# Near keys of linear attention: high and low scores in one matmul of 512 columns, and a sum of two bank halves over 256 columns

## The chip, the core and the metric

The kernel runs on one NeuronCore of one Trainium2 chip. The metric is the device time of one execution in microseconds (us). Each time below is that of one program launch; the profile is one more execution, taken by the hardware profiler.

## What is computed

The input has 4 sequences of 256 tokens with 512 features. A linear attention with 32 heads of 128 features follows, then a sigmoid gate with RMS norm, an output projection, a layer norm, a small mixture of low-rank experts beside a dense layer, and a second layer norm. The part that matters here, per head and batch:

```python
qkv = silu(hidden @ qkv_w.T)                       # q, k, v of each head, 128 features
scores = einsum('bhnd,bhmd->bhnm', cq, ck) * diag_decay   # in blocks of 32 tokens
intra  = einsum('bhnm,bhmd->bhnd', scores, cv)
inter  = einsum('bhnd,bhde->bhne', cq * q_decay, kv)      # kv: the running state
attn   = intra + inter
xf = attn * rsqrt(mean(attn * attn) + EPS)         # over all heads of a token
out = sigmoid(hidden @ gate_w.T) * norm_w * xf @ out_w.T
```

The kernel doesn't keep the running state. A batch has 256 tokens, so it makes the whole decayed score matrix of a head: 128 near keys against 256 queries and 128 far keys against the last 128 queries.

## The kernel before

**Precision.** Every fp32 product is made from two parts of each operand, a rounded high part and the rest as low part, with three matmuls: high by high, high by low, low by high. ScalarE makes the high parts (helper `copy`, L471, or `silu`, L517), VectorE the low ones (helper `minus`, L1179). So each engine has a piece of work for each operand, and TensorE waits for the low part.

**Blocks.** The 32 heads are worked in 8 groups of 4. A group has blocks named QK0, V0, V1, G01, QK1, G23, QK2, QK3 (query and key projection of one head, values of four, gates of two) and, after V1, the output projection of the group before. Each block is a Strassen-like product of seven terms, `p1` to `p7`, made by `mm3_onto` (L2013 to L2015). Its results go to banks 0 to 3 of PSUM. The attention of a head is woven between the products of the next blocks, in banks 4 to 7, one bank for a batch. It is done in two halves, `e` = 0 and 1, of two batches each.

**The path of a head's half.** `scores(h, e)` on TensorE (L2104 to L2110), decay mask on VectorE (L1251, L1253, L1259), high part on ScalarE and low part on VectorE (both 128x768), then `attention(h, e)` on TensorE: five matmuls a batch. The first three (`mm3`, L2007 to L2009) multiply the near keys' values by the scores of all 256 queries and write columns 0 to 255 of the bank. The fourth (L2124) multiplies the far keys' high values by high and low scores side by side and writes columns 128 to 383: the low part lands in 256 to 383, beside the result. The fifth (L2126) adds the low values. Then a chain of four steps brings the result together:

- ScalarE, `part(h, e)`: copies columns 256 to 383 of both banks into the buffer `sq` (in the profile L471, `sq<-ps 128x256`). It waits for `att_done` of TensorE and for `sq_added` of GpSimd, because `sq` is still being read by the half before.
- VectorE, `add_part(h, e)` (L1268): adds `sq` to columns 128 to 255 of both banks.
- ScalarE, `square(h, e)` (L629): squares the 512 results into the same `sq`. GpSimd adds them to `sqacc` (L1927, `add_squares`), which frees `sq`.
- VectorE, `gated(h, e)` (L1280; L1532 in the last group): multiplies by the gate into `y`, which raises `y_done`. `scores` of the next head into these banks wait for it.

**Queues.** The order on each engine is written out by hand, block by block (functions `qk0`, `v0`, `v1`, `qk1`, ... for each engine), and each engine works its list strictly in order. In `qk1` and `qk2` ScalarE has after `part(h, 1)` the copy of the next head's values (`values_hi`, L471, `vh<-v`), the silus of the next head's q and k, and `square(h, 1)`. VectorE has `add_part(h, 1)`, the low values (`values_lo`, `vl<-v,vh`), the sums `c22_add` and `c12_add` (L1209, L1218), `gated(h, 1)` and the low parts of k (`k1_low`, `k0_low`), for which the next `scores(h + 1, 0)` wait. GpSimd makes the sums of weight blocks for the Strassen terms (L1884, L1887, L1891) from what DMA brings, and `add_squares` in between. `v0` and `v1` have `add_part` of the group's last head ahead of `sums_lo(g, "oa", "A")`, and a little later `sums_lo(g, "ob", "A")`, for which the output projection waits.

Of the kernel before, what the change touches and what calls it, by code (L numbers as in the profile page):

```python
# [14 lines left out]
P = 128  # L15
BATCH, SEQ, HID = 4, 256, 512
# [6 lines left out]
W = 512  # L23
U = 256
SC = SEQ + P
# [96 lines left out]
def added_no(g, name, j):  # L122

    return len(OUT_ADDS) * (g - 1) + OUT_ADDS.index((name, j)) + 1
# [26 lines left out]
def build(nc, stream, xt, x, decay, norm_w, base_b, lora_router, router_b, expert_map, ident_in, ones_in, fresh_in, out):  # L151
    ctx = ExitStack()
    with ctx:
        def sb(name, shape, dt=FP32):
            return ctx.enter_context(nc.sbuf_tensor(name, shape, dt))

        def sem(name):
            return ctx.enter_context(nc.semaphore(name))
# [11 lines left out]
        vh = sb("vh", [P, TT, P], FP32R)  # L170
        vl = sb("vl", [P, TT, P], FP32R)
        s2 = sb("s2", [P, 2, BATCH, SC], FP32R)
        sh, sl = s2[:, 0, :, :], s2[:, 1, :, :]
# [8 lines left out]
        sq = sb("sq", [P, W])  # L182
# [90 lines left out]
        att_part, att_full = sem("att_part"), sem("att_full")  # L273
# [28 lines left out]
        def att_banks(e, c0, c1):  # L302

            return ps[:, S_B + 2 * e:S_B + 2 * e + 2, c0:c1]

        def by_batch(ap):
            return ap.rearrange("p (b n) -> p b n", b=2)
# [161 lines left out]
        def _(act):  # L469
            def copy(dst, src, **kw):  # L470
                return nc.scalar.activation(dst, src, ACT.Copy, **kw)  # L471

            def sums_hi(g, name, part):

                m = load_no(g, name)
                act.wait_ge(t_sum, load_no(g, name) - 2)
                wait_free(act, g, name, part)
                u0, u1 = (0, 3) if part == "A" else (3, 7)
                runs = pieces(g, name, u0, u1)
                for i, (slot, before, n) in enumerate(runs):  # L480
                    ins = copy(wh[:, slot:slot + n, :], stage[:, m % 2, u0 + before:u0 + before + n, :])
                    if i == len(runs) - 1:
                        ins.then_inc(t_hi, 1)
# [138 lines left out]
            def part(h, e):  # L622
                act.wait_ge(att_done, 2 * h + e + 1)
                act.wait_ge(sq_added, 2 * h + e)
                copy(by_batch(sq[:, 0:SEQ]), att_banks(e, SEQ, SC)).then_inc(att_part, 1)

            def square(h, e):
                act.wait_ge(att_full, 2 * h + e + 1)
# [158 lines left out]
            def qk0(g):  # L787
                n, h = block_no(g, QK0), HG * g
                k0_full(n - 1, h - 1)
                u2_copy(n)  # L790
                q1_out(n - 1, h - 1)
                k1_full(n - 1, h - 1)
                part(h - 2, 0)
                p5_copy(n)
                square(h - 2, 0)
                u3_copy(n)
                sums_hi(g, "vb", "A")
                part(h - 2, 1)
                values_hi(h - 1)
                square(h - 2, 1)  # L800
                sums_hi(g, "va", "B")
                q0_out(n, h)
                sums_hi(g, "vb", "B")
                scores_hi(h - 1, 0)
                k1_out(n, h)
# [370 lines left out]
        def _(dve):  # L1176
# [88 lines left out]

            def add_part(h, e):
                dve.wait_ge(att_part, 2 * h + e + 1)
                nc.vector.tensor_tensor(att_banks(e, P, SEQ), att_banks(e, P, SEQ), by_batch(sq[:, 0:SEQ]), ALU.add)\  # L1268
                    .then_inc(att_full, 1)

            def gated(h, e):
# [117 lines left out]
            def qk0(g):  # L1389
                n, h = block_no(g, QK0), HG * g  # L1390
                k0_low(n - 1, h - 1)
                add_part(h - 2, 0)
                q1_low(n - 1, h - 1)
                gated(h - 2, 0)
                k1_low(n - 1, h - 1)
                sums_lo(g, "vb", "A")
                add_part(h - 2, 1)
                gated(h - 2, 1)
                mask(h - 1, 0)
                c22_add(n)  # L1400
                mask_sum(h - 1, 0)
                sums_lo(g, "va", "B")
                c12_add(n)
                values_lo(h - 1)
                scores_lo(h - 1, 0)
                sums_lo(g, "vb", "B")

            def v0(g):
                n, h = block_no(g, V0), HG * g
                q0_low(n - 1, h)  # L1410
                mask(h - 1, 1)
                k1_low(n - 1, h)
                mask_sum(h - 1, 1)
                k0_low(n - 1, h)
                q1_low(n - 1, h)
                scores_lo(h - 1, 1)
                add_part(h - 1, 0)
                c22_add(n)
                gated(h - 1, 0)
                c12_add(n)  # L1420
# [583 lines left out]
        def _(pe):  # L2004
            def mm3(dst, wt, mv_, start, stop):

                nc.tensor.matmul(dst, wt[0], mv_[0], start=start, stop=False)  # L2007
                nc.tensor.matmul(dst, wt[0], mv_[1], start=False, stop=False)  # L2008
                return nc.tensor.matmul(dst, wt[1], mv_[0], start=False, stop=stop)  # L2009
# [103 lines left out]
            def attention(h, e):  # L2113
                pe.wait_ge(v_lo, h + 1)
                pe.wait_ge(s_lo, 2 * h + e + 1)
                if h > 0 and h % HG == 0:
                    pe.wait_ge(o_added, added_no(h // HG, "c21" if e else "c12", 1))
                for b in (2 * e, 2 * e + 1):
                    bank = ps[:, S_B + b, :]
                    mm3(bank[:, 0:SEQ], (vh[:, 2 * b, :], vl[:, 2 * b, :]),  # L2120
                        (sh[:, b, 0:SEQ], sl[:, b, 0:SEQ]), True, False)


                    nc.tensor.matmul(bank[:, P:SC], vh[:, 2 * b + 1, :], s2[:, :, b, SEQ:SC],  # L2124
                                     start=False, stop=False, skip_group_check=True)
                    last = nc.tensor.matmul(bank[:, P:SEQ], vl[:, 2 * b + 1, :], sh[:, b, SEQ:SC],  # L2126
                                            start=False, stop=True)
                last.then_inc(att_done, 1)

            def out_product(g, i, j, bank, start, stop):  # L2130
# [102 lines left out]
            def qk0(g):  # L2233
                n, h = block_no(g, QK0), HG * g
                p1(n)
                p4(n - 1)
                attention(h - 2, 0)
                p5(n)
                p6(n)
                attention(h - 2, 1)  # L2240
                p2(n)
                scores(h - 1, 0)
                p7(n)
                p3(n)
                scores(h - 1, 1)

            def v0(g):
                n, h = block_no(g, V0), HG * g
                p1(n)
                p4(n - 1)  # L2250
                p5(n)
                p6(n)
                if g > 0:
                    attention(h - 1, 0)
                p2(n)
                p7(n)
                p3(n)
# [374 lines left out]
```

## Time and profile before

| | us |
|---|---|
| median of 3 runs | 996.95 |
| lowest and highest | 996.23, 997.51 |
| the profiled execution | 996.55 |
| its span | 994.8 |

| engine | busy, us | share | instructions |
|---|---|---|---|
| TensorE, matmuls (PE) | 982.2 | 99% | 5569 |
| TensorE, weight loads (PEld) | 860.6 | 87% | 5569 |
| VectorE (DVE) | 815.9 | 82% | 1122 |
| ScalarE (ACT) | 710.0 | 71% | 1197 |
| GpSimd (POOL) | 456.0 | 46% | 426 |

The granted clock of TensorE was 0.998 of full speed over the span. In the rows, a matmul's duration runs from its issue to its modelled end, so matmuls that follow each other overlap: what one costs in a full queue is the distance from its start to the start of the next. A row's name is output <- inputs, a form is output size <- input size; the line of a copy is that of its helper (L471 for all plain ScalarE copies). 1.6 to 1.8 us of an execution lie outside the span.

### The profile page before, as it was taken

Reading aid. Unit: us, or ns where it says so; the run is one execution under the profiler, and the core shown is the slowest. Engines: PE = TensorE matmul, PEld = TensorE weight load, DVE = VectorE, ACT = ScalarE, POOL = GpSimd, SP = SyncE. Lnnn points to the kernel's source line nnn. Section 1 sums busy time; section 2 is a strip of 40 time slices with the busy share of each in tenths; the row PEclk is TensorE's granted clock in tenths of the full one; section 3 lists DMA queues with packets and bytes.
Section 4 is the critical chain, followed back from the end, with each engine's and each line's share of the span. In section 5 each row is a group of like instructions: output and inputs, shape, how many; then the busy total and the mean of one; then the engine's idle time right before and its main releaser. Section 6 shows DMA issues by size and latency. Waiting matters only on the chain.

```text
span 994.8 us, 15911 instructions
## 1 busy us (share of the span) xinstructions
PE 982.2 (99%) x5569; PEld 860.6 (87%) x5569; DVE 815.9 (82%) x1122; ACT 710.0 (71%) x1197; POOL 456.0 (46%) x426
## 2 busy tenths in 40 slices
PE   8999999999999999999999999999999999999997
PEld 7878998889888898889988898888988899888896
DVE  6767887888967988779877889778887788899876
ACT  6677885788767785778857887677857788587653
POOL 1352564446453463534644464544635345531423
PEclk9999999999999999999999999999999999999999
DMA  6121111201121112212112111110122121110402
GB/s 211 30 64 46 64 48 48 71 30 52 51 65 51 35 47 72 63 44 66 45 55 66 30 52 51 64 51 30 51 72 64 38 73 38 56 52 22 159 12 85
DMA packets 52799, 57.78 MB, mean 58 GB/s; under 512 B 4336, under 2 KB 47728, under 8 KB 52720
## 3 DMA queue, kind: packets, MB, share of 16 engines
q1 hardware_dynamic: 52720, 56.77, 18.3%
q8 instruction: 45, 0.74, 0.3%
q14 instruction: 34, 0.28, 0.1%
HBM read 54.65 MB, written 2.10 MB: 57 GB/s over the span
## 4 chain that ended last, share of the span: by engine, by line
PE 93%; DMA 1%; ACT 1%; DVE 1%; issue 1%; POOL 1%; SPq 0%; POOLq 0%; ACTq 0%; DVEq 0%
PE ps L2013 25%; PE ps L2014 24%; PE ps L2015 24%; PE ps L2007 3%; PE ps L2009 3%; PE ps L2008 3%; PE ps L2110 2%; PE ps L2104 2%; PE ps L2106 2%; PE ps L2105 1%; PE ps L2124 1%; DMA stage<-stream 1%; PE ps L2108 1%; PE ps L2126 1%; DVE wl L1179 1%
## 5 line engine op out<-in xcount | busy, mean ns | idle before, releaser
L1884 POOL TENSOR_TENSOR stage<-stage 128x512 f32<-128x512 f32 x75 | 106.6, 1421 | 354.6 <-DMA stage<-stream 290.8
L2013 PE MATMUL ps<-xh,wh 128*128 128x512 f32 x658 | 260.0, 395 | 1.4 <-ACT stg L517 1.0
L2014 PE MATMUL ps<-xl,wh 128*128 128x512 f32 x658 | 257.0, 391 | 0.0
L2015 PE MATMUL ps<-xh,wl 128*128 128x512 f32 x658 | 256.2, 389 | 0.0
L1179 DVE TENSOR_TENSOR wl<-stage,wh 128x768 fp32r<-128x768 f32 (+3 forms) x183 | 201.3, 1117 | 28.4 <-ACT wh L471 27.7
L471 ACT ACTIVATE wh<-stage 128x768 fp32r<-128x768 f32 (+3 forms) x183 | 147.4, 833 | 17.8 <-POOL stage L1891 8.1
L2015 PEld LDWEIGHTS ps<-xh,wl 128*128 128x128 f32 x658 | 123.6, 188 | 26.8
L2013 PEld LDWEIGHTS ps<-xh,wh 128*128 128x128 f32 x658 | 123.7, 188 | 25.4 <-issue 1.8
L1927 POOL TENSOR_TENSOR sqacc<-sqacc,sq 128x512 f32<-128x512 f32 x64 | 92.8, 1451 | 110.9 <-ACT sq L629 110.9
L2014 PEld LDWEIGHTS ps<-xl,wh 128*128 128x128 f32 x658 | 123.7, 188 | 21.9
L471 ACT ACTIVATE ps<-ps 128x512 f32<-128x512 f32 x150 | 87.0, 584 | 65.0 <-PE ps L2015 65.0
L2013 PE MATMUL ps<-wh,xh 128*128 128x256 f32 (+1 forms) x423 | 122.8, 290 | 0.0
L2015 PE MATMUL ps<-wh,xl 128*128 128x256 f32 (+1 forms) x423 | 121.7, 288 | 0.0
L2014 PE MATMUL ps<-wl,xh 128*128 128x256 f32 (+1 forms) x423 | 121.5, 287 | 0.0
L1891 POOL TENSOR_TENSOR stage<-stage 128x256 f32<-128x256 f32 x75 | 81.0, 1080 | 5.9
L2013 PEld LDWEIGHTS ps<-wh,xh 128*128 128x128 f32 x423 | 80.8, 191 | 0.4
L2014 PEld LDWEIGHTS ps<-wl,xh 128*128 128x128 f32 x423 | 80.9, 191 | 0.3
L2015 PEld LDWEIGHTS ps<-wh,xl 128*128 128x128 f32 x423 | 80.8, 191 | 0.0
L1887 POOL TENSOR_TENSOR stage<-stage 128x256 f32<-128x256 f32 x75 | 68.4, 912 | 5.9
L1179 DVE TENSOR_TENSOR s<-ps,s 128x768 fp32r<-128x768 f32 x64 | 61.0, 953 | 10.1 <-ACT s L471 9.9
L471 ACT ACTIVATE s<-ps 128x768 fp32r<-128x768 f32 x64 | 51.7, 808 | 22.3 <-DVE ps L1259 22.2
L1253 DVE TENSOR_TENSOR ps<-ps,dec 128x768 f32<-128x768 f32 x64 | 61.1, 955 | 0.0
(224 smaller groups left out, 2320.9 us busy)
## 6 DMA issues: line engine op xcount, KB each, us to landing
stage<-stream SPq DMA_DIRECT2D x75, 384.0 KB, 3.4
stage<-stream SPq DMA_DIRECT2D x79, 128.0 KB, 2.1
dec<-decay SPq DMA_DIRECT2D x32, 192.0 KB, 2.4
stage<-stream SPq DMA_DIRECT2D x13, 256.0 KB, 3.1
acc<-xt SPq DMA_DIRECT2D x8, 256.0 KB, 6.0
v<-x SPq DMA_DIRECT2D x8, 256.0 KB, 5.8
out<-v SPq DMA_DIRECT2D x8, 256.0 KB, 2.0
y_home<-lora_router SPq DMA_DIRECT2D x1, 512.0 KB, 5.1
```

The lines of the kernel that those rows point to most:

```text
L471: return nc.scalar.activation(dst, src, ACT.Copy, **kw)
L1179: return nc.vector.tensor_tensor(dst, full, f32(hi), ALU.subtract)
L1253: nc.vector.tensor_tensor(att_banks(e, 0, SC), att_banks(e, 0, SC), dec[:, h % 2, :].unsqueeze(1).broadcast_to([P, 2, SC]), ALU.mult)\
L1884: nc.gpsimd.tensor_tensor(stage[:, s, 1:5:3, :], stage[:, s, 0:6:5, :], stage[:, s, 7:8, :].broadcast_to([P, 2, U]), ALU.add).then_inc(t_p ...
L1887: nc.gpsimd.tensor_tensor(stage[:, s, 2, :], stage[:, s, 1, :], stage[:, s, 5, :], ALU.add)\
L1891: nc.gpsimd.tensor_tensor(stage[:, s, 6, :], stage[:, s, 2, :], stage[:, s, 3, :], ALU.add)\
L1927: nc.gpsimd.tensor_tensor(sqacc[:, e, :], sqacc[:, e, :], sq[:, :], ALU.add).then_inc(sq_added, 1)
L2007: nc.tensor.matmul(dst, wt[0], mv_[0], start=start, stop=False)
L2008: nc.tensor.matmul(dst, wt[0], mv_[1], start=False, stop=False)
L2013: nc.tensor.matmul(dst, wt[0], mv_[0], start=start, stop=False, skip_group_check=True)
L2014: nc.tensor.matmul(dst, wt[0], mv_[1], start=False, stop=False, skip_group_check=True)
L2015: return nc.tensor.matmul(dst, wt[1], mv_[0], start=False, stop=stop, skip_group_check=True)
```

## The change

It touches the attention's matmuls, the copy `part` and the sum `add_part`.

- TensorE: the three matmuls on near keys become two. The first has 512 columns: the high values by high and low scores side by side, into the whole bank, high into 0 to 255 and low into 256 to 511. The second adds the low values by the high scores into 0 to 255. The far keys' matmul of 256 columns now writes two pieces of 128 columns, 128 to 255 and 384 to 511. The last is as before. In all four matmuls a batch instead of five, with the same 1152 columns.
- ScalarE: `part` copies 256 columns of each of two banks, 512 in all, instead of 256 in all.
- VectorE: `add_part` adds 512 columns instead of 256.

```diff
@@ ScalarE
             def part(h, e):
                 act.wait_ge(att_done, 2 * h + e + 1)
                 act.wait_ge(sq_added, 2 * h + e)
-                copy(by_batch(sq[:, 0:SEQ]), att_banks(e, SEQ, SC)).then_inc(att_part, 1)
+                copy(by_batch(sq[:, :]), att_banks(e, SEQ, W)).then_inc(att_part, 1)
@@ VectorE
             def add_part(h, e):
                 dve.wait_ge(att_part, 2 * h + e + 1)
-                nc.vector.tensor_tensor(att_banks(e, P, SEQ), att_banks(e, P, SEQ), by_batch(sq[:, 0:SEQ]), ALU.add)\
+                nc.vector.tensor_tensor(att_banks(e, 0, SEQ), att_banks(e, 0, SEQ), by_batch(sq[:, :]), ALU.add)\
                     .then_inc(att_full, 1)
@@ TensorE, attention(h, e)
                 for b in (2 * e, 2 * e + 1):
                     bank = ps[:, S_B + b, :]
-                    mm3(bank[:, 0:SEQ], (vh[:, 2 * b, :], vl[:, 2 * b, :]),
-                        (sh[:, b, 0:SEQ], sl[:, b, 0:SEQ]), True, False)
-
-
-                    nc.tensor.matmul(bank[:, P:SC], vh[:, 2 * b + 1, :], s2[:, :, b, SEQ:SC],
+                    parts = bank.rearrange("p (a n) -> p a n", a=2)
+                    nc.tensor.matmul(parts, vh[:, 2 * b, :], s2[:, :, b, 0:SEQ], start=True, stop=True)
+                    nc.tensor.matmul(bank[:, 0:SEQ], vl[:, 2 * b, :], sh[:, b, 0:SEQ], start=False, stop=False,
+                                     skip_group_check=True)
+                    nc.tensor.matmul(parts[:, :, P:SEQ], vh[:, 2 * b + 1, :], s2[:, :, b, SEQ:SC],
                                      start=False, stop=False, skip_group_check=True)
                     last = nc.tensor.matmul(bank[:, P:SEQ], vl[:, 2 * b + 1, :], sh[:, b, SEQ:SC],
-                                            start=False, stop=True)
+                                            start=False, stop=True, skip_group_check=True)
```

TensorE's list before, around an attention half in a V0 block; the second batch begins in the last row.

```order
L2015 MATMUL ps<-wh,xl 128x256
L2007 MATMUL ps<-s,vh 128x256 [waits s_lo,v_lo]
L2008 MATMUL ps<-s,vh 128x256
L2009 MATMUL ps<-s,vl 128x256
L2124 MATMUL ps<-s,vh 128x256
L2126 MATMUL ps<-s,vl 128x128
L2007 MATMUL ps<-s,vh 128x256
```

The same place now.

```order
L2015 MATMUL ps<-wh,xl 128x256
L2121 MATMUL ps<-s,vh 128x512 [waits s_lo,v_lo]
L2122 MATMUL ps<-s,vl 128x256
L2124 MATMUL ps<-s,vh 128x2x128
L2126 MATMUL ps<-s,vl 128x128
L2121 MATMUL ps<-s,vh 128x512
```

Nothing else moved on TensorE; each attention half is two instructions shorter. On ScalarE and VectorE the lists stand as before, and only the size in the rows of `part` (`sq<-ps`, now 128x512) and of `add_part` (L1268, now 128x2x256) differs.

## Rows read from the trace of the kernel before

**Rows 1.** The page, part 1: busy time, share of the span, instructions.
```profile
PE 982.2 (99%) x5569; PEld 860.6 (87%) x5569; DVE 815.9 (82%) x1122; ACT 710.0 (71%) x1197; POOL 456.0 (46%) x426
```

**Rows 2.** Timeline of PE: start, duration (us), engine, line, operation, names, form.
```profile
53.04 0.39 PE L2013 MATMUL ps<-xh,wh 128*128 128x512 f32 x1
...
53.72 0.28 PE L2007 MATMUL ps<-s,vh 128*128 128x256 f32 x1
...
54.20 0.22 PE L2126 MATMUL ps<-s,vl 128*128 128x128 f32 x1
54.26 0.34 PE L2007 MATMUL ps<-s,vh 128*128 128x256 f32 x1
54.43 0.28 PE L2008 MATMUL ps<-s,vh 128*128 128x256 f32 x1
...
54.85 0.45 PE L2013 MATMUL ps<-xh,wh 128*128 128x512 f32 x1
55.13 0.40 PE L2014 MATMUL ps<-xl,wh 128*128 128x512 f32 x1
```

**Rows 3.** Groups by line and form, whole span: count | busy us, mean ns.
```profile
L629 ACT ACTIVATE sq<-ps 128x512 f32<-128x512 f32 x64 | 38.3, 599 | 21.3 <-DVE ps L1268 21.2
L1209 DVE TENSOR_TENSOR stg<-ps,stg 128x512 f32<-128x512 f32 x61 | 41.7, 684 | 14.7 <-PE ps L2015 14.7
L1268 DVE TENSOR_TENSOR ps<-ps,sq 128x256 f32<-128x256 f32 x64 | 27.5, 430 | 39.9 <-ACT sq L471 39.6
L471 ACT ACTIVATE sq<-ps 128x256 f32<-128x256 f32 x64 | 24.4, 382 | 25.8 <-POOL sqacc L1927 18.4 <-PE ps L2126 7.4
```

**Rows 4.** Timelines of ACT, POOL, DVE and PE, block QK1 of group 2.
```profile
291.88 0.39 ACT L471 ACTIVATE sq<-ps 128x256 f32<-128x256 f32 x1 [1.26 <-POOL sqacc L1927]
...
292.65 1.30 POOL L1884 TENSOR_TENSOR stage<-stage 128x512 f32<-128x512 f32 x1 [0.86 <-DMA stage<-stream]
...
293.25 1.78 DVE L1179 TENSOR_TENSOR vl<-v,vh 128x1024 fp32r<-128x1024 f32 x1 [0.52 <-ACT vh L471]
...
297.35 1.89 DVE L1179 TENSOR_TENSOR k<-stg,k 128x512 fp32r<-128x512 f32 x2
...
297.53 0.63 ACT L517 ACTIVATE stg<-stg 128x512 f32<-128x512 f32 x1
...
299.34 0.35 PE L2104 MATMUL ps<-q,k 128*128 128x256 f32 x1
```

**Rows 5.** Timelines of POOL, DVE and PE, block QK1 of group 4.
```profile
525.78 1.23 DVE L1179 TENSOR_TENSOR vl<-v,vh 128x1024 fp32r<-128x1024 f32 x1 [0.52 <-ACT vh L471]
...
525.83 1.78 POOL L1887 TENSOR_TENSOR stage<-stage 128x256 f32<-128x256 f32 x1
...
529.45 1.88 DVE L1179 TENSOR_TENSOR k<-stg,k 128x512 fp32r<-128x512 f32 x2
...
531.66 0.28 PE L2104 MATMUL ps<-q,k 128*128 128x256 f32 x1
```

**Rows 6.** Timelines of POOL and DVE, block V1 of group 3.
```profile
359.74 0.43 DVE L1268 TENSOR_TENSOR ps<-ps,sq 128x256 f32<-128x256 f32 x1 [1.61 <-ACT sq L471]
...
361.06 1.29 POOL L1906 TENSOR_TENSOR y<-y,y_home 128x512 f32<-128x512 f32 x1
...
361.57 1.60 DVE L1179 TENSOR_TENSOR wl<-stage,wh 128x768 fp32r<-128x768 f32 x1
```

**Rows 7.** Timelines of DVE and PE, block QK0 of group 6.
```profile
692.50 0.69 DVE L1280 SCALAR_TENSOR_TENSOR y<-y,ps 128x512 f32<-128x512 f32 x1 [0.67 <-ACT sq L629]
...
693.34 0.36 PE L2104 MATMUL ps<-q,k 128*128 128x256 f32 x1 [0.18 <-DVE y L1280]
```

**Rows 8.** Timelines of DVE and PE, the last block of the last group.
```profile
919.46 0.43 DVE L1268 TENSOR_TENSOR ps<-ps,sq 128x256 f32<-128x256 f32 x1
...
919.80 0.68 DVE L1209 TENSOR_TENSOR stg<-ps,stg 128x512 f32<-128x512 f32 x1
...
920.86 0.39 PE L2013 MATMUL ps<-xh,wh 128*128 128x512 f32 x1
```

## The prediction

> **What bounds the kernel now.** I read the page's busy times first, then TensorE's timeline in steady stretches for what a matmul costs in a full queue, then the groups by line and form for the two instructions that grow, and last, for each wait of TensorE, the timelines of the engines that it waits for. TensorE is busy for 982.2 of 994.8 us, VectorE for 815.9, ScalarE for 710.0 [rows 1]. So TensorE's list is the time: a matmul less is a gain at once, and work added to another engine costs only where TensorE already waits for it, or comes within a few tenths of a microsecond of doing so. The reader should see two things in the rows: the pace of TensorE, and how little room there is at a handful of places.
>
> **The gain: one matmul fewer a batch.** Start to start, three matmuls of 512 columns take 53.72 - 53.04 = 0.68 us, 0.227 each. The four of 256 columns from 53.72 to 54.20 take 0.12 each, the one of 128 takes 0.06 [rows 2]. So 512 columns in one piece cost 0.227, in two pieces 0.24: the merge gives 0.013 us. A head has four batches: 32 x 4 = 128 merges, 1.7 us. The first matmul after the one of 128 columns costs 0.05 more (54.26 to 54.43, 0.17 instead of 0.12); one of 512 columns in that place also costs 0.05 more (54.85 to 55.13, 0.28 instead of 0.227) [rows 2]. That cancels. The far keys' matmul has the same 256 columns, but writes two pieces with a gap between. No row of TensorE shows such an output. Its bounds are nothing, as for a contiguous one of 256, and the 0.05 us of the nearest irregularity, which would be 128 x 0.05 = 6.4 us. A gain is excluded, since the columns are the same. I take nothing, because the input side of this same matmul already comes in two pieces and keeps the pace of 0.12.
>
> The Trainium skill says in "TensorE: Matmul & The Clock Gate", section "Back-to-back issue gap", that an isolated warm matmul takes N / 2.4 + 2.5 ns. By that a merge saves 2.5 ns, 0.3 us in all, and the forecast would come out 1.4 us higher. The row shows 13 ns, and I go by the row.
>
> **The cost: two longer steps in each half.** There are 64 halves. ScalarE's `part` takes 0.382 us for 256 columns; its square of 512 columns from PSUM into the same buffer takes 0.599 [rows 3]. I take 0.58 to 0.60: +0.20 us, 13 us of ScalarE over the kernel. VectorE's `add_part` takes 0.430; a sum of 512 columns with one input in PSUM takes 0.684 [rows 3]: +0.25 us, 16 us of VectorE. The link from `att_done` to the squares grows by 0.45 us. And since `part` of half 1 waits until GpSimd has added the squares of half 0, a delay of half 0 is handed on to half 1 through GpSimd: there it can reach 0.45 + 0.20 = 0.65 before `add_part`. If all of it came through at the places below, it would cost about 8 us; all of it hidden, nothing. What decides is what else the delayed instructions are waiting for.
>
> **Block QK1, where scores wait for the low part of k.** `part(h, 1)` starts at 291.88, released by GpSimd's squares; the copy of the values follows it, and VectorE's `values_lo` starts at 293.25, released by that copy [rows 4]. From there VectorE is busy without a gap up to `k0_low`, the second of the two at 297.35, which ends at 299.24; the scores start at 299.34 [rows 4]. So TensorE waits for this chain, and `values_lo` would start some 0.5 us later (0.3 handed on through the squares, 0.2 from the copy). But `values_lo` takes 1.78 us here and 1.23 in group 4 [rows 4, 5]. GpSimd's L1884 runs from 292.65 to 293.95, released by a DMA, and VectorE's instruction stands still behind it. A start at 293.75 instead of 293.25 then ends at the same time. What is left is ScalarE: its last silu of k ends at 298.16 [rows 4], 0.4 us before `k0_low` starts (299.24 - 0.68 = 298.56); 0.5 later makes 0.1 us. So I take 0.1 in group 2 and nothing in group 1, which looks alike with a little more room.
>
> In groups 0, 3 and 6 `sums_hi` is late for another reason (its sums come late from GpSimd), so nothing is handed on and only the longer copy, 0.2 us, reaches `k0_low`, through ScalarE: 0.2 each. Group 4 goes the other way. `values_lo` starts at 525.78, 0.05 ahead of GpSimd's L1887 at 525.83, and makes that wait: 1.78 us [rows 5]. Half a microsecond later GpSimd is first, and VectorE waits for it: about 0.9 us, of which the following blocks of GpSimd give some back. I take 0.6; `k0_low` ends at 531.33 and the scores start at 531.66, so 0.25 us is room [rows 5]. That leaves 0.3. Group 5 has `values_lo` just ahead of GpSimd too, but its `k0_low` is itself held up by GpSimd later, which takes the delay up: nothing. The last group has this block in another order, 0.2. Sum: 0.1 + 3 x 0.2 + 0.3 + 0.2 = 1.2 us. Block QK2 has the same chain with 0.5 us of room: 0.2 us for all groups.
>
> The Trainium skill says in "SBUF — State Buffer", section "Who interferes with whom", that VectorE and GpSimd share an exclusive pair of ports and that the one which issues second stands fully still. By that rule the trace agrees: 1.78 us against 1.23 for the same instruction.
>
> **Start of the output projection.** It waits for `sums_lo(g, "ob", "A")` on VectorE, some 10 us after `add_part` of the group's last half (359.74), with hardly a gap between [rows 6]. By then the delays of both halves have added up to some 0.9 us. `sums_lo(g, "oa", "A")` at 361.57 takes 1.60 us because GpSimd's L1906 runs until 362.35 [rows 6]; started at 362.5, it loses only about 0.25, and the few idle tenths before the next steps take that up. I take 0.1 us for each of six groups. In group 7 the two engines meet the other way around, and I take 0.85, the full delay. Sum 1.45 us.
>
> **Single places.** In group 6 the scores of block QK0 wait for `gated`, which ends at 693.19 and releases TensorE at 693.34; ahead of it stand `add_part` and the square [rows 7]. The +0.25 of `add_part` passes whole: 0.26. In the last block `c22_add` stands behind `add_part` of the last half: it starts at 919.80 and ends at 920.48, and TensorE needs it at 920.86 [rows 8]. The delay there is the handed-on 0.45, plus 0.20, plus 0.25: 0.9 us, less 0.34 of room: 0.56. Two halves earlier another 0.16. Sum 1.0 us.
>
> **The sum.** -1.7 + 1.2 + 0.2 + 1.45 + 1.0 = +2.1 us. On the profiled execution's 996.55 that is 998.7; the median of the runs is 0.4 higher, so I forecast **999.1 us**, 0.2% above.
>
> **The rivals.**
> *All hidden.* Between the attention and the next wait stand GpSimd locks and DMA waits that set the end of VectorE's work anyway. For it: groups 1 and 5 and the start of the output projection in most groups. Against it: rows 7 and 8, where no such lock stands. With the last block's costs alone it is 996.95 - 1.7 + 1.0 = 996.3; without these 995.3.
> *Not swallowed (slower).* The delays of 0.45 to 0.65 pass whole, because VectorE comes behind GpSimd instead of ahead of it as in group 4. The place is `values_lo` in QK1 and `sums_lo(g, "oa", "A")` in V1. Price: 0.5 x 8 in QK1, 0.35 x 7 at the projection, single places 1.5: 8 - 1.7 = +6.3, 1003.2 us. It decides from the point where `values_lo` starts after GpSimd's next step has begun: rows 4 have 0.7 us of that step left, rows 5 none.
> *The scattered output costs.* At 0.05 us a matmul the gain of 1.7 becomes a loss of 4.7: 1005.5. Nothing in the trace speaks for it.
> *Not what it says.* That TensorE keeps five matmuls is excluded by the order of instructions.
>
> **Chances.** Forecast with its own range 997.5 to 1001: 0.45. All hidden, 995.2 to 997.5: 0.28. Not swallowed, 1001 to 1006: 0.22. Scattered output or something else: 0.05. A measurement of this kernel can tell about 0.2% from no change, 2.0 us: below 994.9 is faster, above 998.9 slower. Faster would need more than the whole 1.7 us: 0.06. Slower: a little over half of the forecast's case, all of the third, most of the last: 0.50. The same: 0.44. For 8 in 10 the range takes in most of the second and third cases: 995.6 to 1003.5.
>
> **What would show it.** In the changed profile: TensorE's matmuls 128 fewer; L2121 at 0.22 to 0.28 start to start and the scattered L2124 at 0.12; `part` at 0.58 to 0.60 and `add_part` at 0.68 us. `values_lo` in QK1 of group 2 should end when it does now, relative to the attention before it, and be shorter by its later start; in group 4 it should be longer, about 1.7. The waits of the scores L2104 should grow by 1 to 2 us in all, and the last block's L2013 should start 0.5 us late after its predecessor. I am wrong if L2124 shows 0.17, if `add_part` stays well below 0.6, or if waits of TensorE grow by more than 5 us or shrink.

## The result, and the profile after

| | before | after |
|---|---|---|
| median, us | 996.96 (4 runs) | 1005.92 (4 runs) |
| lowest and highest | 996.23, 997.51 | 1005.38, 1006.95 |
| span of the profiled execution | 994.8 | 1004.7 |

The ratio is 1.0094 (95% interval 1.0082 to 1.0107): 0.9% slower, 9.0 us. The forecast was 999.1 with a range up to 1003.5.

The page of the changed kernel, busy times, and from its groups by line and form the two longer steps (third and fourth row), their two neighbours, and the group of TensorE's matmuls that begin a product of 256 columns:

```profile
PE 988.3 (98%) x5441; PEld 855.6 (85%) x5441; DVE 828.9 (83%) x1122; ACT 723.1 (72%) x1197; POOL 450.5 (45%) x426
```

```profile
L629 ACT ACTIVATE sq<-ps 128x512 f32<-128x512 f32 x64 | 38.4, 601 | 28.9 <-DVE ps L1268 28.8
...
L1209 DVE TENSOR_TENSOR stg<-ps,stg 128x512 f32<-128x512 f32 x61 | 41.7, 683 | 13.9 <-PE ps L2015 13.9
...
L1268 DVE TENSOR_TENSOR ps<-ps,sq 128x512 f32<-128x512 f32 x64 | 44.6, 696 | 49.8 <-ACT sq L471 49.8
...
L471 ACT ACTIVATE sq<-ps 128x512 f32<-128x512 f32 x64 | 38.2, 596 | 26.4 <-POOL sqacc L1927 19.0 <-PE ps L2126 7.1
...
L2013 PE MATMUL ps<-wh,xh 128*128 128x256 f32 x392 | 112.8, 288 | 4.6 <-ACT ps L471 4.6
```

TensorE has 128 matmuls fewer. `part` takes 0.596 us instead of 0.382, `add_part` 0.696 instead of 0.430 [rows 3]: both as forecast. The last row is the news: TensorE now stands 4.6 us for a ScalarE copy at the begin of a product in the value blocks. No row of that kind and size stood in the profile before.

TensorE's timeline of an attention half in a full queue, with what begins behind it:

```profile
290.20 0.39 PE L2121 MATMUL ps<-s,vh 128*128 128x512 f32 x1
290.43 0.28 PE L2122 MATMUL ps<-s,vl 128*128 128x256 f32 x1
290.54 0.28 PE L2124 MATMUL ps<-s,vh 128*128 128x256 f32 x1
290.66 0.22 PE L2126 MATMUL ps<-s,vl 128*128 128x128 f32 x1
290.72 0.46 PE L2121 MATMUL ps<-s,vh 128*128 128x512 f32 x1
291.01 0.28 PE L2122 MATMUL ps<-s,vl 128*128 128x256 f32 x1
...
291.31 0.45 PE L2013 MATMUL ps<-xh,wh 128*128 128x512 f32 x1
```

The scattered L2124 costs 0.12 start to start, like a contiguous one. But the half takes 291.31 - 290.20 = 1.11 us, against 54.85 - 53.72 = 1.13 before [rows 2]; over all halves the medians are 1.113 and 1.123. The merged matmul costs 0.23 behind one of 512 columns and 0.29 behind the one of 128, where the two of 256 before cost 0.17 + 0.12 = 0.29 too. So the merges give 0.01 a half, 0.6 to 0.8 us in all, not 1.7.

Where the time went is read by how much later TensorE comes by in the changed kernel. It jumps in one block above all. Block V1 of group 3, timelines of GpSimd, VectorE, ScalarE and TensorE (compare [rows 6]):

```profile
364.89 1.29 POOL L1906 TENSOR_TENSOR y<-y,y_home 128x512 f32<-128x512 f32 x1
366.14 1.30 POOL L1884 TENSOR_TENSOR stage<-stage 128x512 f32<-128x512 f32 x1
```

```profile
364.05 0.70 DVE L1268 TENSOR_TENSOR ps<-ps,sq 128x512 f32<-128x512 f32 x1 [1.83 <-ACT sq L471]
...
366.15 2.11 DVE L1179 TENSOR_TENSOR wl<-stage,wh 128x768 fp32r<-128x768 f32 x1
368.18 0.41 DVE L1251 TENSOR_TENSOR ssum<-ps,dec 128x256 f32<-128x256 f32 x1
...
374.10 1.75 DVE L1179 TENSOR_TENSOR wl<-stage,wh 128x768 fp32r<-128x768 f32 x1
```

```profile
369.97 0.81 ACT L471 ACTIVATE s<-ps 128x768 fp32r<-128x768 f32 x1 [1.69 <-DVE ps L1259]
370.67 0.59 ACT L471 ACTIVATE ps<-ps 128x512 f32<-128x512 f32 x1
```

```profile
370.47 0.28 PE L2015 MATMUL ps<-wh,xl 128*128 128x256 f32 x1
371.32 0.39 PE L2013 MATMUL ps<-wh,xh 128*128 128x256 f32 x1 [0.57 <-ACT ps L471]
...
375.91 0.50 PE L2013 MATMUL ps<-yh,wh 128*128 128x512 f32 x1
```

GpSimd in the kernel before, behind the L1906 of [rows 6]:

```profile
362.31 2.01 POOL L1884 TENSOR_TENSOR stage<-stage 128x512 f32<-128x512 f32 x1
```

Before, `sums_lo(g, "oa", "A")` came to VectorE at 361.57, while GpSimd's L1906 ran until 362.35, and took 1.60 us [rows 6]. It was ahead of L1884, and L1884 took 2.01 instead of 1.30. Now it comes at 366.15, 0.01 us after GpSimd has begun its next instruction, L1884, and takes 2.11. Decay mask, ScalarE's `scores_hi` (idle for 1.69 until then) and, behind that on ScalarE, the copy `u3_copy` follow; TensorE's `p7` waits for it: it starts at 371.32, where a full queue would start it 0.12 behind the matmul at 370.47, at 370.59. Then the output projection starts at 375.91, released by the low sums of ob that end at 375.85. Counted in TensorE's progress, `p7` costs 0.82 us in each of six groups and 1.3 in the last one, the projection's start 0.24 in six: 6 x 0.82 + 1.3 + 6 x 0.24 = 7.7 us. The prediction had 1.45 there. In the last group the two engines meet otherwise, and the full delay passes.

The single places, timelines of VectorE and TensorE: block QK0 of group 6, then the last block [rows 7, 8].

```profile
699.32 0.69 DVE L1280 SCALAR_TENSOR_TENSOR y<-y,ps 128x512 f32<-128x512 f32 x1 [0.66 <-ACT sq L629]
...
700.15 0.35 PE L2104 MATMUL ps<-q,k 128*128 128x256 f32 x1 [0.96 <-DVE y L1280]
```

```profile
929.87 0.68 DVE L1209 TENSOR_TENSOR stg<-ps,stg 128x512 f32<-128x512 f32 x1
...
930.61 0.50 PE L2013 MATMUL ps<-xh,wh 128*128 128x512 f32 x1 [0.49 <-DVE stg L1209]
```

TensorE's wait in group 6 is 0.96 instead of 0.18: 0.78 more. The last block costs 0.78, and the scores two halves earlier 0.70.

### The profile page after: what moved, and what is told of

Read it like the earlier page. It is cut to its first block and busy times, and to the rows that moved or that the text cites. A ratio compares the mean times of both kernels' runs of the same rounds, so it can differ in the third digit from the quotient of the medians.

```text
span 1004.7 us, 15655 instructions
## 1 busy us (share of the span) xinstructions
PE 988.3 (98%) x5441; PEld 855.6 (85%) x5441; DVE 828.9 (83%) x1122; ACT 723.1 (72%) x1197; POOL 450.5 (45%) x426
## 5 line engine op out<-in xcount | busy, mean ns | idle before, releaser
L1884 POOL TENSOR_TENSOR stage<-stage 128x512 f32<-128x512 f32 x75 | 99.9, 1332 | 358.6 <-DMA stage<-stream 293.2
L1179 DVE TENSOR_TENSOR wl<-stage,wh 128x768 fp32r<-128x768 f32 (+3 forms) x183 | 204.3, 1134 | 24.2 <-ACT wh L471 23.4
L1268 DVE TENSOR_TENSOR ps<-ps,sq 128x512 f32<-128x512 f32 x64 | 44.6, 696 | 49.8 <-ACT sq L471 49.8
L1891 POOL TENSOR_TENSOR stage<-stage 128x256 f32<-128x256 f32 x75 | 80.7, 1076 | 5.9
L1887 POOL TENSOR_TENSOR stage<-stage 128x256 f32<-128x256 f32 x75 | 71.5, 954 | 5.9
```

What stands on the lines that cost most here:

```text
L1179: return nc.vector.tensor_tensor(dst, full, f32(hi), ALU.subtract)
L1268: nc.vector.tensor_tensor(att_banks(e, 0, SEQ), att_banks(e, 0, SEQ), by_batch(sq[:, :]), ALU.add)\
L1884: nc.gpsimd.tensor_tensor(stage[:, s, 1:5:3, :], stage[:, s, 0:6:5, :], stage[:, s, 7:8, :].broadcast_to([P, 2, U]), ALU.add).then_inc(t_p ...
L1887: nc.gpsimd.tensor_tensor(stage[:, s, 2, :], stage[:, s, 1, :], stage[:, s, 5, :], ALU.add)\
L1891: nc.gpsimd.tensor_tensor(stage[:, s, 6, :], stage[:, s, 2, :], stage[:, s, 3, :], ALU.add)\
```

## The experiments

All ratios are to the kernel before on the same chip, with 95% intervals; its medians there were 996.1 to 996.5. The expectations set theory S against others. S (string and threshold) says that delays add up along the lists of ScalarE and VectorE, and that the price jumps where VectorE comes behind GpSimd's next step in V1. Theory A (additive) says that each longer step has a price of its own.

The profiled executions differ by up to 2 us before the first block begins: TensorE's first block matmul starts at 41.41 us in the changed kernel, 41.48 in the kernel before, 42.66 in e7 and 43.09 in e2. Where a cause is in question, the text below therefore goes by TensorE's lag over a stretch of one execution (how much later it comes by at its end than at its begin, against the kernel before), and not by the whole time. From just ahead of `p7` in V1 to the first matmul of the projection the changed kernel loses 1.0 us in each of groups 1 to 6.

| kernel | median, us | ratio |
|---|---|---|
| e1 matmuls alone | 992.62 | 0.9960 (0.9949 to 0.9972) |
| e2 copy alone | 998.55 | 1.0022 (1.0011 to 1.0032) |
| e3 sum alone | 997.61 | 1.0011 (0.9998 to 1.0024) |
| e4 `u3_copy` first | 1005.95 | 1.0097 (1.0078 to 1.0117) |
| e5 mask first | 1004.63 | 1.0076 (1.0061 to 1.0091) |
| e6 mask first, in before | 997.38 | 1.0008 (0.9997 to 1.0019) |
| e7 copy and sum, old matmuls | 1010.31 | 1.0131 (1.0111 to 1.0151) |
| e8 one half of eight short | 999.87 | 1.0037 (1.0023 to 1.0050) |
| e9 only its copy short | 1000.00 | 1.0042 (1.0027 to 1.0057) |
| e10 new in heads 0, 1 | 996.91 | 1.0011 (1.0002 to 1.0020) |
| e11 new in heads 2, 3 | 999.14 | 1.0040 (1.0027 to 1.0054) |
| e12 sums early | 1000.50 | 1.0045 (1.0030 to 1.0060) |
| e13 sums early, keys first | 1005.72 | 1.0102 (1.0085 to 1.0119) |
| e14 both moves, in before | 996.86 | 1.0006 (0.9997 to 1.0015) |

### Which part costs: e1, e2, e3, e7

e1, the changed kernel with short steps:

```diff
-copy(by_batch(sq[:, :]), att_banks(e, SEQ, W)).then_inc(att_part, 1)
+copy(by_batch(sq[:, 0:SEQ]), att_banks(e, SEQ + P, W)).then_inc(att_part, 1)
-tensor_tensor(att_banks(e, 0, SEQ), att_banks(e, 0, SEQ), by_batch(sq[:, :]), ALU.add)
+tensor_tensor(att_banks(e, P, SEQ), att_banks(e, P, SEQ), by_batch(sq[:, 0:SEQ]), ALU.add)
```

> The four new matmuls, with copy and sum as short as before (256 columns: the copy takes columns 384 to 511, the sum adds them to 128 to 255). Left out: the product of high values and low scores of the first 128 queries, which lands in columns 256 to 383 and is added to nothing. If TensorE's part is what the prediction took it for (128 x 0.013 us gained, the scattered output free), the time is 996.95 - 1.7 = 995.3 us (994.5 to 996). If the new matmuls themselves cost something that the pitches don't show, it is above 997. The loss of about 9 us must then come from the two longer steps, or not.

e2 and e3, the kernel before with one step longer each (e2's sum, not shown, reads the same 256 columns as before out of the wider copy):

```diff
@@ e2
-copy(by_batch(sq[:, 0:SEQ]), att_banks(e, SEQ, SC)).then_inc(att_part, 1)
+copy(by_batch(sq[:, :]), att_banks(e, SEQ, W)).then_inc(att_part, 1)
@@ e3
-tensor_tensor(att_banks(e, P, SEQ), att_banks(e, P, SEQ), by_batch(sq[:, 0:SEQ]), ALU.add)
+both = att_banks(e, 0, SEQ).rearrange("p b (a n) -> p b a n", a=2)
+low = by_batch(sq[:, 0:SEQ]).unsqueeze(2).broadcast_to([P, 2, 2, P])
+tensor_tensor(both, both, low, ALU.add)
```

> The kernel before, with only ScalarE's copy lengthened to 512 columns (the sum still uses 256 of them). Theory S (string and threshold): from block QK2 to the start of the projection ScalarE and VectorE hand work to each other with hardly a gap, delays add up, and the low sums of oa in V1 come only 0.2 us later against GpSimd; VectorE is then still first in line when GpSimd's L1906 ends, so no port swap: 998 us (997 to 999.5). Theory A (additive: each of the two longer steps has its own price in proportion to its length): the 10.7 us between 995.3 and 1005.9 split as 0.21 to 0.27, so +4.7: 1001.6 us.

> The kernel before, with only VectorE's sum lengthened to 512 columns; it adds the low part to columns 0 to 127 too, where it does not belong. Theory S: three longer sums lie on the string, so at V1 VectorE is 0.5 us later against GpSimd, less than the 0.75 of the changed kernel and less than the 0.8 that L1906 has left, so VectorE stays first and the 0.5 us of port swap is not paid: about 0.4 a group and 0.6 in the singles, 1000.5 us (999 to 1002). Theory A: +6.0: 1003 us. Under S the effects of copy and sum add up to about 5, well under the 10.7 that both have together; under A they add up to 10.7.

e7 has both longer steps together, with the five old matmuls.

> The kernel before with its five matmuls, and copy and sum both of 512 columns (the sum adds the low part to columns 0 to 127 too, where it does not belong). Alone the copy cost 2.1 us and the sum 1.1, and the matmuls alone gained 3.9, together -0.7; the changed kernel loses 9.4. Theory S: it is the two longer steps together that bring VectorE 0.75 us later against GpSimd in V1, behind the begin of L1884, so that it stands for 1.2 us instead of going first; the five old matmuls don't matter for that: 1006 us (1003 to 1008). Rival M: the interaction is with the new matmuls (TensorE 0.2 us a group earlier uses up the last room), and here the two costs only add up: 999.7 us.

Measured against before: matmuls -3.9 us, copy +2.1, sum +1.1 (its interval reaches from nothing to 2.4); both steps together +14.2, the whole change +9.0. The steps cost far more together than apart: theory A, a price for each, falls, and so does rival M, since e7 has the old matmuls. S had the pattern, but only e2 lies in its range: e1 and e3 came out 2.7 and 2.9 us below the expected time, e7 4.3 above it. e7 shows the stall of V1 to the hundredth. GpSimd, VectorE and TensorE in e7, group 3:

```profile
366.53 1.30 POOL L1908 TENSOR_TENSOR y<-y,y_home 128x512 f32<-128x512 f32 x1
367.79 1.30 POOL L1886 TENSOR_TENSOR stage<-stage 128x512 f32<-128x512 f32 x1
```

```profile
367.80 2.10 DVE L1179 TENSOR_TENSOR wl<-stage,wh 128x768 fp32r<-128x768 f32 x1
```

```profile
372.96 0.38 PE L2015 MATMUL ps<-wh,xh 128*128 128x256 f32 x1 [0.55 <-ACT ps L471]
```

In e3 the same sums arrive before the meeting point, and they take less time than before:

```profile
361.12 1.30 POOL L1908 TENSOR_TENSOR y<-y,y_home 128x512 f32<-128x512 f32 x1
362.36 2.03 POOL L1886 TENSOR_TENSOR stage<-stage 128x512 f32<-128x512 f32 x1
```

```profile
362.17 1.06 DVE L1179 TENSOR_TENSOR wl<-stage,wh 128x768 fp32r<-128x768 f32 x1
```

They arrive 0.60 us later than before by the clock and end at the same time: 362.17 + 1.06 = 363.23, before 361.57 + 1.60 = 363.17. The delay is swallowed, and it is GpSimd's L1886 that waits (2.03 instead of 1.30).

The same place gives the reason for the jump. What counts is how far the sums come ahead of GpSimd's next step: 362.31 - 361.57 = 0.74 us in the kernel before, 0.54 in e2, 0.19 in e3, and nothing in e7 (367.80 against 367.79). The copy takes 0.20 of this room and the sum 0.55, and together they use it up. From `p7` to the start of the projection TensorE loses 0.00 in e2 and e3 in groups 2 to 6, and 1.0 in e7 in each of them. With the last group that is 7.3 of the 14.3 us by which e7's profile is longer; 1.2 stand before the first block, and the rest is spread over QK1, QK2 and the single places.

### Which wait: e4, e5, e6

e4 takes the last link away: ScalarE's copy goes first.

```diff
-scores_hi(h, 0)
 u3_copy(n)
+scores_hi(h, 0)
 sums_hi(g, "ob", "A")
```

> The changed kernel, with ScalarE's u3_copy in V1 ahead of scores_hi(h, 0) instead of behind it; in the profile its input is there 2.5 us before it starts, and TensorE's p7 waits 0.72 us for it. Theory O (order): what costs is that u3_copy stands behind scores_hi, so p7 starts 0.7 us earlier and the kernel gets back 6 x 0.7 + 1.3 = 5.6 us: 1000.3 us. Theory S: p7 starts earlier, but VectorE's list up to the low sums of ob is without a gap from add_part on and ends when it did, so the same wait comes up again at p4 (c22_added) and at the projection's start (t_lo): 1005.5 us (1004.5 to 1006).

1005.95: the time is that of the changed kernel. TensorE's `p7` no longer waits, but two products later it does; TensorE and VectorE in e4, group 3:

```profile
374.31 0.39 PE L2013 MATMUL ps<-wh,xh 128*128 128x256 f32 x1 [0.60 <-DVE stg L1209]
```

```profile
373.58 0.68 DVE L1209 TENSOR_TENSOR stg<-ps,stg 128x512 f32<-128x512 f32 x1
```

VectorE has no gap from 366.24 to 376.79 there. It is its list that is late, and the copy was only where the delay came out first. So the theory "order" (O) falls.

The same execution holds the clearest test of the meeting. In groups 2 and 4 the sums come 0.02 to 0.03 us ahead of GpSimd's step instead of behind it; VectorE and GpSimd in e4, group 2:

```profile
250.02 0.96 DVE L1179 TENSOR_TENSOR wl<-stage,wh 128x768 fp32r<-128x768 f32 x1
```

```profile
250.04 2.10 POOL L1884 TENSOR_TENSOR stage<-stage 128x512 f32<-128x512 f32 x1
```

From `p7` to the start of the projection TensorE loses 0.00 us in these two groups, and 1.0 in each of groups 1, 3, 5 and 6, where the sums take 2.09 to 2.10. The lists are the same in all these groups; what differs is who comes first. The whole time doesn't show the two spared groups: this execution's first block begins 1.1 us later than in the changed kernel's profile, and the output block behind group 4 loses another 0.3.

e5 moves the low sums behind the mask, e6 does so in the kernel before.

```diff
 gated(h - 1, 1)
-sums_lo(g, "oa", "A")
 mask(h, 0)
 mask_sum(h, 0)
+sums_lo(g, "oa", "A")
 operand_lo(g, 5)
```

> The changed kernel, with VectorE's low sums of oa in V1 behind the mask of the next head instead of ahead of it. In the changed kernel these sums arrive at 366.15, just after GpSimd's L1884 has begun at 366.14, and take 2.11 us; mask, scores_hi, u3_copy and TensorE's p7 stand behind them. Theory S (string and threshold): mask starts 2 us earlier, p7 no longer waits (0.72 us in six groups, 1.3 in the last), and the sums themselves meet GpSimd for less time, so that the low sums of ob come 0.5 to 0.9 us earlier: of the 1.08 us a group 0.5 to 1.0 comes back, 1000 us (998.5 to 1002.5). Theory W (the wait only moves, as when u3_copy went first): the low sums of ob end when they did, 1005.5 us.

> The same move in the kernel before, as a control. There p7 has 1.1 us of room and the projection's start 0.16, and VectorE goes first after L1906. Theory S: nothing to gain at p7; the projection's start moves by what the changed meeting with GpSimd gives or takes: 996.5 us (995.5 to 998). If the move were simply better everywhere, it would gain here as much as in the changed kernel: 991 us.

e5 got 1.3 us back of the 6 expected: a miss. The meeting moved on with the sums; VectorE in e5:

```profile
367.12 1.42 DVE L1179 TENSOR_TENSOR wl<-stage,wh 128x768 fp32r<-128x768 f32 x1
368.46 1.75 DVE L1179 TENSOR_TENSOR vl<-y_home,vh 128x1024 fp32r<-128x1024 f32 x1
```

1.42 + 1.75 us for the two instructions that took 2.11 + 1.22 in the changed kernel: 0.16 less. `p7` was free, but `p4` and the projection waited: TensorE lost 0.7 in each group from `p7` to the projection's start, instead of 1.0. e6 was level, as expected.

### Length or meeting point: e8, e9, e12

e8 shortens copy and sum in one half of eight; e9 only the copy there. The edit (shown for the copy) takes eight halves of 64: seven stand right ahead of the meeting in V1, the eighth stands in the last block, where there is no such meeting. The expectations count seven.

```diff
+if h % HG == 3 and e == 1:
+    copy(by_batch(sq[:, 0:SEQ]), att_banks(e, SEQ + P, W)).then_inc(att_part, 1)
+else:
     copy(by_batch(sq[:, :]), att_banks(e, SEQ, W)).then_inc(att_part, 1)
```

> The changed kernel, but in one half of eight (the second of each group's last head, in block V1) copy and sum are as short as before; left out there: the product of high values and low scores of the first 128 queries. 0.48 us less on the string just ahead of the low sums of oa. Theory S: these arrive 0.3 us after GpSimd's L1906 instead of 0.75, are first in line for L1884, and both the 0.5 us of stall and the 0.48 us are gone: 7 x 0.9 = 6 us come back, 1000 us (998.5 to 1001.5). Theory A (each half costs its share of the 9 to 13 us): 7 of 64 halves, 1.0 to 1.5 us back: 1004.7 us.

> The changed kernel; in one half of eight (the second of each group's last head, block V1) ScalarE's copy alone is as short as before, VectorE's sum keeps its 512 columns (in these halves it adds the low part of queries 128 to 255 to columns 0 to 127 too, where it does not belong). This takes the two effects of the last run apart, length and port. Theory S: the low sums of oa arrive 0.54 us late against GpSimd instead of 0.75, before L1906 ends, so they are first in line again and stall no longer than in the kernel before: 0.21 + 0.5 us of 7 groups come back, 1001 us (999.5 to 1002.5). Theory L (length only, no threshold): 7 x 0.21 = 1.5 us back, 1004.5 us.

Both give 6 us back; e9 does so with eight copies 0.23 us shorter (0.37 instead of 0.60), 1.8 us of work. Group 3 of e9, GpSimd and VectorE:

```profile
362.78 1.30 POOL L1913 TENSOR_TENSOR y<-y,y_home 128x512 f32<-128x512 f32 x1
364.04 2.02 POOL L1891 TENSOR_TENSOR stage<-stage 128x512 f32<-128x512 f32 x1
```

```profile
363.82 1.07 DVE L1182 TENSOR_TENSOR wl<-stage,wh 128x768 fp32r<-128x768 f32 x1
```

The sums arrive 0.22 us ahead of GpSimd's next step instead of 0.01 behind it, and take 1.07 instead of 2.11. TensorE loses 0.00 us there in groups 2 to 6 in both, instead of 1.0. That the sum's extra 0.27 makes no difference between e8 and e9 is the swallowing again. (e8's profiled execution, 1002.26, was the longest of its seven.)

e12 shortens nothing. It moves the sums ahead of a GpSimd instruction:

```diff
@@ ScalarE, v1
 part(h - 1, 1)
+sums_hi(g, "oa", "A")
 u2_copy(n)
 square(h - 1, 1)
-sums_hi(g, "oa", "A")
@@ VectorE, v1
-gated(h - 1, 1)
 sums_lo(g, "oa", "A")
+gated(h - 1, 1)
 mask(h, 0)
```

> The changed kernel; in V1 ScalarE makes the high sums of oa right behind the copy, ahead of u2_copy and square, and VectorE the low sums ahead of the gate. Nothing is left out. The low sums then arrive at about 364.75 by the trace of the changed kernel, 0.07 us before GpSimd's L1902 ends and 0.14 before its L1906 would begin, so that VectorE goes first and L1906 and L1884 shift behind it. Theory S (it is the meeting with GpSimd): mask starts 1.5 to 1.8 us earlier, all waits of V1 and at the projection's start go: 7 x 1.08 = 7.5 us back, 998.4 us (997 to 1000.5). Theory W (string length alone sets it, as when the mask went first): 0.3 us a group, 1004 us.

1000.5, 5.4 us back of the 9.0. Group 3, VectorE and GpSimd:

```profile
363.73 0.96 DVE L1179 TENSOR_TENSOR wl<-stage,wh 128x768 fp32r<-128x768 f32 x1
```

```profile
363.84 2.00 POOL L1906 TENSOR_TENSOR y<-y,y_home 128x512 f32<-128x512 f32 x1
```

Undisturbed, the sums take 0.96 us, and TensorE loses 0.00 us at this place in groups 2 to 6. With e4, e9 and e12 the meeting point is shown: in e12 the same work, with only the order of arrival changed, is worth 5.4 us. In the last group e12 still waited at `p4` and the projection. No run has the move of V1 alone in the kernel before; e14 below has it together with another and is level.

### Where the delay comes from: e10, e11

Each has the changed kernel's matmuls, copy and sum in two of a group's four heads and the old ones in the others (`h % HG < 2` in e10, `h % HG > 1` in e11).

> Matmuls, copy and sum of the changed kernel in heads 0 and 1 of each group (blocks QK1 and QK2), those of the kernel before in heads 2 and 3 (QK0, V0, V1). Nothing is left out. Theory S: the loss of V1 needs the longer steps of heads 2 and 3; here only what QK1 and QK2 cost is left, 1.4 us by the prediction, against half of the matmuls' gain, 0.85: 997.5 us (996 to 999). Theory A (each half its share): half of the loss, 1001 us.

> The complement: the changed kernel's steps in heads 2 and 3 (QK0, V0, V1), those of before in heads 0 and 1. Nothing is left out. Theory S: the 0.75 us against GpSimd arise in V0 and V1 alone, so the port swap and most of the string are there: 0.8 to 1.0 us a group in V1, the single places of groups 6 and 7: 1003.5 us (1002 to 1005.5). Theory A: 1001 us. If the delay carried over from QK2 were needed for it, this and the run before would both stay below 999.

e10 is 0.6 us slower than before, as S had it. e11 came to 999.1, not 1003.5: a miss. Its executions spread from 997.2 to 1002.8, and its profile says why. Groups 4 and 5 of the same execution, VectorE and GpSimd each:

```profile
478.32 0.96 DVE L1182 TENSOR_TENSOR wl<-stage,wh 128x768 fp32r<-128x768 f32 x1
```

```profile
478.33 2.11 POOL L1891 TENSOR_TENSOR stage<-stage 128x512 f32<-128x512 f32 x1
```

```profile
595.02 2.12 DVE L1182 TENSOR_TENSOR wl<-stage,wh 128x768 fp32r<-128x768 f32 x1
```

```profile
595.02 1.30 POOL L1891 TENSOR_TENSOR stage<-stage 128x512 f32<-128x512 f32 x1
```

At 0.01 us ahead VectorE takes 0.96 and GpSimd 2.11; at a tie VectorE takes 2.12 and GpSimd 1.30. In all six groups of e11 the two starts lie within 0.01 us of each other. VectorE is first in groups 2, 3 and 4, and TensorE loses 0.00 us there; it is second in groups 1, 5 and 6, and TensorE loses 0.8 to 1.0 (in the seventh group the engines meet otherwise). The starts in the trace don't say who wins so near the edge: group 3 is a tie too, and VectorE takes 0.96. e10 still has 0.72 us of the 0.74 of room. So the steps of heads 2 and 3 use the room up alone, to the very edge, where S had expected them to go past it. In the changed kernel's profile all six groups are past it, by 0.01 to 0.03 us. Heads 0 and 1 matter for that: e11's ten executions lie at 997.2 to 1002.8, the changed kernel's four at 1005.4 to 1007.0. How their steps supply these hundredths no run shows.

### The key blocks: e13, e14

e13 is e12 with the low parts of k ahead of `gated` on VectorE, and ScalarE's high parts of k ahead of the next high sums; e14 has both moves in the kernel before.

```diff
@@ VectorE, qk1 and qk2
 c12_add(n)
-gated(h, 1)
 k1_low(n, h + 1)
 k0_low(n, h + 1)
+gated(h, 1)
@@ ScalarE, qk1 (qk2 alike)
-sums_hi(g, "qk2", "B")
 k1_out(n, h + 1)
 k0_out(n, h + 1)
+sums_hi(g, "qk2", "B")
```

> The kernel of the run before, and in QK1 and QK2 the low parts of k ahead of the gate on VectorE, and the high parts of k ahead of the next high sums on ScalarE. Nothing is left out. If QK1 and QK2 cost what the prediction took for them, 1.4 us, and the kernel before itself waits there in some groups (0.1 to 0.8 us each), this gains 2 to 3 us more: 996 us (994.5 to 998), about the kernel before or a little under. If these waits only move on to V1, it gains nothing: 998.4 us.

> Both moves in the kernel before, as a control. In V1 there is nothing to gain (0.16 us and more of room), in QK1 and QK2 what TensorE waits there: 1 to 2 us: 995 us (993.5 to 997). The difference to the run above then says what the change is worth where its longer steps are covered: between the -1.7 us that the prediction took for the matmuls and the -3.9 us of the matmuls alone, plus the single places of groups 6 and 7.

e13 lost 5.2 us to e12: a miss. TensorE's waits at `k0_lo` shrank by up to 0.2 us each, and one in QK0 grew by 0.8 in nearly every group; TensorE in e13, group 3:

```profile
348.14 0.36 PE L2104 MATMUL ps<-q,k 128*128 128x256 f32 x1 [0.64 <-DVE y L1280]
```

By the rows, ScalarE's sums (1.05 us in QK2) now stand right ahead of `u2_copy` and `q1_out`, and that delay seems to run on through QK3 to `gated` in QK0; no run tests this. e14 is level with before; 1 to 2 us faster was expected. None of the 14 kernels computes everything and is faster than the kernel before.

## Why the prediction was wrong, point by point

- **Durations and the scattered output: right.** 0.596 and 0.696 us (0.58 to 0.60 and 0.68 were forecast), L2124 at 0.12.
- **The gain of the merges: too high.** -1.7 was predicted; the trace shows 0.01 a half, 0.6 to 0.8 us. The step that failed is "That cancels": behind the matmul of 128 columns the merged one costs 0.29, not 0.277, as much as the two that it replaces, and every second merged matmul stands there. The sum was 1 us too low by that. Of the Trainium skill's 2.5 ns ("TensorE: Matmul & The Clock Gate", section "Back-to-back issue gap") and the 13 ns that I took from a row, the measured 5 to 6 ns a merge is nearer to the first.
- **QK1: right in single groups, wrong in sum.** +1.2 us was forecast; TensorE's lag over these blocks shrank by 1.8. In group 2 its scores L2104 start 2.95 us later than before, its attention ends 2.97 later: nothing lost, 0.1 was forecast. But that is not by the step that the prediction named. `values_lo` came 0.4 us later and took 1.48 instead of 1.78 [rows 4], behind GpSimd's L1887 and no longer behind L1884, which had ended. The rest came back at `k1_low`: before, it took 1.29 us while GpSimd added squares, now 0.68, since the squares are over by then. Group 4 lost 0.25 (0.3 forecast), with GpSimd's steps at other times than those assumed and 1.48 for `values_lo` instead of some 1.7: the agreement is luck. In groups 3, 5 and 7 the lag shrank by 0.9, 0.5 and 1.0 us, where 0.2, nothing and 0.2 of loss were forecast.
- **QK2, QK0 and V0: too small.** QK2 cost 0.9 to 1.0, not 0.2. In QK0 and V0 another 0.1 to 0.2 a group comes in, 1.5 us in all besides group 6, for which the prediction had no term. e10 puts QK1 and QK2 together at a loss of 0.6 us, net of half the matmuls' gain.
- **The start of the projection: the step that failed.** 0.1 in six groups and 0.85 in one, 1.45 us, against 7.7. The failed step is "started at 362.5, it loses only about 0.25". The prediction placed the sums 0.15 us after L1906's end at 362.35 and looked no further. GpSimd starts its next instruction there without a gap, so an arrival after that end waits for the whole of it. The kernel before, e9 and e11 measure the curve: arrival 0.79, 0.26 and 0.05 us before that end gives 1.60, 1.07 and 0.96 us; 0.02 to 0.04 us before it, when L1884 has begun, gives 2.09 to 2.11. The Trainium skill says in "SBUF — State Buffer", section "Who interferes with whom", that the shared pair of ports is an exclusive lock and the engine that issues second is blocked. The trace agrees: 0.96 alone, 2.11 behind an instruction of 1.30. I had used that rule for the swallowing and not for the step behind it.
- **The accumulated delay: too small.** 0.9 us was taken for the delay at these sums. The trace has 366.15 - 361.57 = 4.58, less 3.28 by which TensorE itself was late: 1.30. GpSimd's steps, which the prediction held in place, came 366.14 - 362.31 = 3.83 later, less 3.28: 0.55. So against GpSimd, which decides here, VectorE lost 0.75. By e10 and e11 nearly all of that arises in heads 2 and 3, and heads 0 and 1 add some hundredths at most.
- **Single places: right in kind, short in size.** 0.78 in group 6 (0.26), 0.78 in the last block (0.56), 0.70 two halves earlier (0.16): the delays there were larger than taken.
- **The rival "not swallowed"** named the place, V1, and the mechanism, with 1003.2 us (1001 to 1006). It priced it at 0.35 a group; it was 1.06, and 1.3 in the last. That 1005.9 lies in its range is in part luck: 4 us of its sum stand in QK1, where nothing was lost in sum.

What stays open: e1 gained 3.9 us, and the matmuls account for 0.6 to 0.8. In its profile the rest are shorter waits in the key and output blocks (the largest in QK1 of groups 3, 5 and 7, as in the changed kernel), as here in group 5 (VectorE's low parts of k, before and in e1):

```profile
645.47 2.55 DVE L1179 TENSOR_TENSOR k<-stg,k 128x512 fp32r<-128x512 f32 x2
```

```profile
643.80 1.89 DVE L1179 TENSOR_TENSOR k<-stg,k 128x512 fp32r<-128x512 f32 x2
```

Before, GpSimd's squares run beside them; in e1 its sums had come 1.1 us earlier from a DMA, and they don't meet as long. Why all executions of e1 share this was not tried, so of its 3.9 us some 3 have no tested cause.

## What to carry to other kernels

Where two engines share an exclusive resource and each has a list without gaps, price a delay by the instruction that the other engine starts next, not by the end of the one that runs: up to that end the delay is free, and past it one full instruction is due. A cost found for each part alone says little about both (2.1 and 1.1 us apart, 14.2 together), and a wait taken away at its last link comes back at the next one as long as the late engine's list is unchanged. A gain of a few nanoseconds an instruction should be read from a whole period of the pattern, its irregular neighbours included.

## What the runs showed of the hardware

- A matmul that writes two pieces of 128 columns with a gap costs no more than a contiguous one of 256: 0.12 us.
- VectorE's sum of 768 columns in SBUF takes 0.96 us alone; behind a GpSimd instruction of 1.30 it takes 2.11, and GpSimd's takes 2.11 behind VectorE's. Where the two starts lie within 0.01 us, either can be first (e11: in three groups of six VectorE).
- VectorE's instructions with an operand in PSUM (512 columns) kept their 0.67 to 0.70 us beside a running GpSimd instruction: only those with all operands in SBUF were seen to stand.
